# Gated mixing in a two-layer convolution kernel: one image per tile against two images per tile

## The chip, the core and the metric

The kernel runs on one core of one Trainium2 chip. The metric is device time in microseconds (us), taken from the start of the program to its end on that core; lower is better.

## The reference

The input `x` is (8, 64, 256, 256) in float32: 8 images of 64 channels. Two layers follow each other, each as `x = x + layer(groupnorm(x))`.

- Layer 0 shifts four quarters of the channels of two projections by one pixel (one projection first along rows, the other first along columns), weighs them by a softmax gate that is computed for each image from sums over the image, projects the result by a 64x64 matrix, and multiplies it by `sigmoid(scale * x + bias) * x`. All linear parts fold into one small matrix for each image and each of four one-pixel shifts. What is left per pixel is: four shifted 64x64 products, summed; plus a constant; times the sigmoid; plus 1; times the centred input.
- Layer 1 keeps 64x32 Fourier modes of each image, mixes the channels of each mode by complex weights, transforms back and adds.

## The kernel before

The program is a row of stages with a barrier between them: statistics of `x` (DVE and ACT read all of it), a chain of small matrix steps that ends in `wall` (the folded matrices) and `params` (scales and biases), the **mixing stage** (layer 0, lines 511 to 741), a short stage that turns the sums of the mixing stage into the second norm (745 to 793), the forward transform, the mixing of modes, and the backward transform with the last addition. Only the mixing stage and the addresses of what it writes change here.

**The mixing stage before.** It takes one image after the other, 16 rows at a time: 128 tiles. Of a tile, `mix_x` (`XT`, four buffers) holds 17 rows of 257 columns on 128 partitions. The lower 64 partitions hold the 64 channels shifted by one column, the upper 64 the same channels shifted by one row. A matmul with 128 input partitions so takes two of the four shifts at a time, and `m` in 0, 1 takes both pairs. Two output halves (even and odd rows, `par`) fill the 128 partitions of PSUM.

- SP (sync) loads the two halves of a tile by a transfer each onto 64 partitions (564, 567), four tiles ahead, and waits for `conv_done` and `sig_done` of the tile that had the buffer.
- DVE copies what the other half needs: `up` (686), eight rows to the upper partitions, and `down` (691), eight rows to the lower ones, two tiles ahead. It then has the two fused steps of the tile: `gated` (721) reads the matmul's PSUM and the sigmoid, and `mix_out` (730) reads two SBUF tiles and also sums its result. In every second tile it makes half of the centred input (699).
- POOL pads the two edge columns after `down` (589), by two small operations.
- PE runs 16 products of 512 columns (32 matmul instructions) per tile (617), after `padded` and after `gated` of two tiles before has freed the PSUM half.
- ACT makes the centred input (640, one or two halves), the sigmoid (648), issues the store of the finished tile (661) and squares it for the second norm (666).

The order on each engine is written out by hand: in step n, DVE runs up(n+2), gated(n), down(n+2), mix_out(n) and at every second tile centre(n+2); ACT runs gate(n+2), store(n), square(n). The 32 tiles of an image pair are one body of a hardware loop (three rounds, and a last one apart).

Of the kernel before, what the change touches and what calls it, by code (L numbers as in the profile page):

```python
# [42 lines left out]
MR = 2 * SP_  # L43

LAYOUT = ((0, 0, 2), (1, 0, 1), (0, 1, 0), (1, 1, 3))
PITCH = W + 1
# [10 lines left out]
def constants():  # L57
# [23 lines left out]
    put("spread", spread.reshape(P, -1))  # L81
    put("sign", np.stack([np.where(p < C, 1.0, -1.0)] * 2, 1))
# [31 lines left out]
def program(nc, x, w1m, b1m, w2m, b2m, sa1, sa2, gamma, beta, wr1, wi1, wr2, wi2, const, out):  # L114
    top = ExitStack()
    with top:
# [3 lines left out]
        x1 = nc.dram_tensor("x1_scratch", (B, H, C, W), F32, kind="Internal").ap()  # L120
# [7 lines left out]
        x1_rows = x1.rearrange("b h c w -> h b (c w)")  # L128
# [21 lines left out]
        params = sb(top, "params", [P, B + 1, 4])  # L150
        wall = sb(top, "wall", [P, B + 1, P])
# [7 lines left out]
        with ph:  # L159
# [40 lines left out]
            with nc.Block() as block:  # L200
# [12 lines left out]
                def _(pool):  # L213
# [13 lines left out]
                    pool.memset(wall[:, B, :], 0.0)  # L227
                    pool.memset(params[:, B, :], 0.0)
# [283 lines left out]
        with ph:  # L512
            NX = 4
            XT = [sb(ph, f"mix_x{i}", [P, MR + 1, PITCH]) for i in range(NX)]
            XC = [sb(ph, f"centred{i}", [P, SC]) for i in range(NX)]
            G = [sb(ph, f"gated{i}", [P, SC]) for i in range(NX)]
            XO = [sb(ph, f"mix_out{i}", [P, SC]) for i in range(2)]
            SQ = sb(ph, "square", [P, SC])
            one = sb(ph, "one", [P, MR + 1])
            wcur = [sb(ph, f"wcur{i}", [P, P]) for i in range(2)]  # L520
            pcur = [sb(ph, f"pcur{i}", [P, 6]) for i in range(2)]
            loaded = [sem(f"mix_loaded{i}") for i in range(NX)]
            stored = [sem(f"mix_stored{i}") for i in range(2)]
            one_set = sem("mix_one_set")
            doubled, padded, batch_ready = sem("mix_doubled"), sem("mix_padded"), sem("mix_batch_ready")
            xc_done, sig_done, conv_done, sq_done = (sem("mix_" + n) for n in ("xc", "sig", "conv", "sq"))
            h_done, o_done, xc_dve = sem("mix_h"), sem("mix_o"), sem("mix_xc_dve")
            NB = H // MR
            NI = 2 * NB
            ITER = B // 2  # L530

            x1_par = x1.rearrange("b (r e) c w -> b (e c) r w", e=2)

            def split(n):

                return n % 2 == 1

            def loaded_by(i, n):

                q, t = n % NX, n % NB  # L540
                edge = 16 if q in (0, NX - 1) else 0
                batch = NB // NX * 32 + edge
                return i * (2 * batch) + n // NB * batch + (t // NX + 1) * 32 + (edge if q == 0 or t == NB - 1 else 0)

            def iterations(engine, body):

                with engine.Fori(0, ITER - 1) as i:
                    body(i, False)
                body(ITER - 1, True)

            with nc.Block() as block:
                @block.sync
                def _(sp):
                    with sp.Fori(0, ITER) as i:
                        for n in range(NI):
                            ch = bass.ds((i * 2 + n // NB) * C, C)
                            t, xt = n % NB, XT[n % NX]


                            sp.wait_ge(conv_done, i * NI + n + 1)  # L560
                            sp.wait_ge(sig_done, i * NI + n + 1)
                            r0 = t * MR - 1
                            lo = max(r0, 0)
                            sp.dma_start(xt[0:C, lo - r0:MR // 2 + 1, 1:W + 1],
                                         x_rows[ch, lo:r0 + MR // 2 + 1, :]).then_inc(loaded[n % NX], 16)
                            hi = min(r0 + MR + 2, H)
                            sp.dma_start(xt[C:P, MR // 2:hi - r0 - 1, 0:W],
                                         x_rows[ch, r0 + 1 + MR // 2:hi, :]).then_inc(loaded[n % NX], 16)
# [800 lines left out]
```

## Time and profile before

| what | value |
|---|---|
| median of 3 runs | 3113.48 us (3108.65 to 3118.16) |
| the profiled execution's own time | 3114.35 us |
| its span, first to last instruction | 3112.7 us |
| busy in the span: PE, DVE, ACT, POOL | 72%, 65%, 42%, 24% |
| mean granted TensorE clock | 0.930 |

The span is 1.65 us shorter than the execution's own time, which lies 0.9 us over the median. Busy shares are means over stages with different limits, so the profile is to be read stage by stage: the mixing stage lasts from about 380 us to 1462 us of the span.

### The profile page before, as it was taken

To read this page: it belongs to the slowest core of one execution; us is meant where nothing else is said; L and a number is where in the kernel's file an instruction comes from. 1 tells how busy PE (TensorE), PEld (TensorE's weight loads), DVE (VectorE), ACT (ScalarE), POOL (GpSimd) and SP (SyncE) were. 2 spreads that over 40 slices of the span, in tenths; PEclk is the share of its full clock that TensorE was granted. 3 is DMA by queue.
4 is the path that set the end of the run, shared out by engine and by line. 5 is a ranking of instruction groups with operands and counts; after the bars stand their busy time and mean duration, and the time that the engine had idled before them with its cause. 6 is when DMAs were issued, how large, how long until landed. Compare 5 with 4: busy or idle time off the path is not lost. (4 is left out here: it accounts for less than half of the span.)

```text
span 3112.7 us, 38323 instructions
## 1 busy us (share of the span) xinstructions
PE 2255.8 (72%) x12960; PEld 1076.6 (35%) x12960; DVE 2025.2 (65%) x2317; ACT 1302.1 (42%) x1470; POOL 757.3 (24%) x477
## 2 busy tenths in 40 slices
PE   0000288888889889896899898965555989988884
PEld 0000123222223223232345444534555444444442
DVE  8999689989999999997665555640000454544442
ACT  1111078878887888886332222310001222212220
POOL 1000023222323232322655454510000111111111
PEclk9999899999999999998999999987888999998987
DMA  9999299999999999997877676739999999999999
GB/s 402 428 428 428 70 254 264 269 249 276 269 267 257 273 275 267 270 271 215 346 258 260 238 259 243 258 95 347 355 342 317 362 384 395 394 378 409 401 376 351
DMA packets 456398, 949.63 MB, mean 305 GB/s; under 512 B 16608, under 2 KB 377744, under 8 KB 410928
## 3 DMA queue, kind: packets, MB, share of 16 engines
q1 hardware_dynamic: 250720, 619.62, 61.8%
q10 hardware_dynamic: 169984, 192.95, 19.5%
q0 software_dynamic: 35536, 134.84, 11.5%
q8 instruction: 113, 1.85, 0.2%
q14 instruction: 45, 0.37, 0.0%
HBM read 653.75 MB, written 293.60 MB: 304 GB/s over the span
## 5 line engine op out<-in xcount | busy, mean ns | idle before, releaser
L617 PE MATMUL psum<-mix_x,wcur 128*64 128x512 f32 x4096 | 938.1, 614 | 148.6 <-POOL mix_x L589 137.4
L617 PEld LDWEIGHTS psum<-mix_x,wcur 128*64 128x64 f32 x4096 | 311.9, 139 | 774.2 <-issue 564.8
L1227 PE MATMUL psum<-tab_irow_icol_sign,inv_t 128*128 128x512 f32 x1024 | 497.0, 609 | 15.7 <-DVE weights_or_rows L1322 15.1
L589 POOL TENSOR_TENSOR mix_x<-mix_x,one 64x17 f32<-64x17 f32 x256 | 324.0, 1266 | 745.6 <-DVE mix_x L691 738.1
L640 ACT ACTIVATE centred<-mix_x,pcur 64x2048 f32<-64x2048 f32 x192 | 384.2, 2001 | 205.2 <-POOL mix_x L589 188.5
L1322 DVE TENSOR_TENSOR weights_or_rows<-weights_or_rows,psum 128x1024 f32<-128x1024 f32 x224 | 272.7, 1221 | 265.7 <-PE psum L1227 228.5
L983 ACT ACTIVATE fwd_rows<-psum 128x512 f32<-128x512 f32 x256 | 152.2, 598 | 414.6 <-PE psum L869 384.8
L730 DVE SCALAR_TENSOR_TENSOR mix_out<-gated,centred 128x2048 f32<-128x2048 f32 x128 | 293.6, 2294 | 39.4 <-issue 35.2
L264 DVE BATCH_NORM_STATS2 stats<-stat_x 128x6 f32<-128x512 f32 x512 | 305.4, 676 | 13.4 <-DMA stat_x<-x 13.0
L721 DVE SCALAR_TENSOR_TENSOR gated<-psum,pcur,gated 128x2048 f32<-128x2048 f32 x128 | 300.9, 2351 | 18.0 <-PE psum L617 16.4
L1052 DVE COPY fwd_cols<-psum 128x136 f32<-128x136 f32 x512 | 154.6, 394 | 237.8 <-PE psum L880 236.7
L869 PE MATMUL psum<-fwd_sum,tab_ident_frow_fcol 128*64 128x512 f32 x512 | 282.5, 635 | 28.4 <-POOL fwd_diff L1077 18.5
L1291 ACT ACTIVATE inv_t<-psum 128x256 f32<-128x256 f32 x256 | 98.4, 384 | 477.3 <-PE psum L1218 477.3
L869 PE MATMUL psum<-fwd_diff,tab_ident_frow_fcol 128*64 128x512 f32 x512 | 282.8, 636 | 0.0
L1077 POOL TENSOR_TENSOR fwd_diff<-fwd_x 128x2048 f32<-128x2048 f32 x48 | 224.3, 4673 | 239.1 <-PE psum L869 205.6
L648 ACT ACTIVATE gated<-centred,pcur 128x2048 f32<-128x2048 f32 x128 | 268.2, 2095 | 9.6 <-DVE centred L699 1.8
L1202 PE MATMUL psum<-weights_or_rows,modes_or_terms 128*16 128x64 f32 x4096 | 170.3, 354 | 135.3 <-DMA modes_or_terms<-modes_in 111.8
L1227 PEld LDWEIGHTS psum<-tab_irow_icol_sign,inv_t 128*128 128x128 f32 x1024 | 199.5, 196 | 164.8 <-issue 146.1
L666 ACT ACTIVATE square<-mix_out 128x2048 f32<-128x2048 f32 x128 | 242.4, 1894 | 3.6 <-DVE mix_out L730 3.6
L296 PE MATMUL psum<-s_ones_dmask_spread_npix,w1d 128*64 128x128 f32 x1 | 0.4, 396 | 333.7 <-PEq L200 333.7
L1218 PE MATMUL psum<-tab_irow_icol_sign,modes_or_terms 128*128 128x256 f32 x512 | 159.7, 396 | 97.1 <-ACT modes_or_terms L1285 97.1
L1334 POOL DMA_DIRECT2D out<-weights_or_rows x112 | 98.7, 886 | 463.6 <-DMA out<-weights_or_rows 229.3
(185 smaller groups left out, 1982.4 us busy)
## 6 DMA issues: line engine op xcount, KB each, us to landing
mix_x<-x SPq DMA_DIRECT2D x240, 576.0 KB, 8.0
stat_x<-x SPq DMA_DIRECT2D x64, 2048.0 KB, 13.0
x_scratch<-mix_out ACTq DMA_DIRECT2D x128, 1024.0 KB, 9.1
weights_or_rows<-x_scratch SPq DMA_DIRECT2D x112, 1024.0 KB, 10.9
out<-weights_or_rows POOLq DMA_DIRECT2D x112, 1024.0 KB, 16.5
fwd_x<-x_scratch SPq DMA_DIRECT2D x96, 1024.0 KB, 6.8
x_tile<-x_scratch SPq DMA_DIRECT2D x46, 1024.0 KB, 8.0
weights_or_rows<-L_conv_w_real SPq DMA_DIRECT2D x8, 4096.0 KB, 34.3
```

The lines of the kernel that those rows point to most:

```text
L264: last = nc.vector.bn_stats(stats[:, at:at + 6], XT[t % NX][:, q * 512:(q + 1) * 512])
L589: last = nc.gpsimd.tensor_tensor(XT[n % NX][h, :, to], XT[n % NX][h, :, of], one[h, :], ALU.mult)
L617: last = nc.tensor.matmul(bank(k * 4 + q, 512, C, par * C), wcur[j][:, m * C:(m + 1) * C], XT[n % NX][:, r0:r0 + 3:2, m:m + W], start=(m = ...
L640: last = nc.scalar.activation(XC[n % NX][h, :].rearrange("p (r w) -> p r w", w=W), XT[n % NX][h, 1:MR:2, 1 - half:1 - half + W], ACT.Ident ...
L648: nc.scalar.activation(G[n % NX][:, :], XC[n % NX][:, :], ACT.Sigmoid, bias=pcur[j][:, 1:2], scale=pcur[j][:, 0:1]).then_inc(sig_done, 1)
L666: nc.scalar.activation(SQ[:, :], XO[k][:, :], ACT.Square, accum_out=sqs[:, bass.ds(i * NI + n, 1)]).then_inc(sq_done, 1)
L721: nc.vector.scalar_tensor_tensor(out=G[n % NX][:, :], in0=psum[:, k * SC:(k + 1) * SC], scalar=pcur[j][:, 3:4], in1=G[n % NX][:, :], op0=A ...
L730: nc.vector.scalar_tensor_tensor(out=XO[k][:, :], in0=G[n % NX][:, :], scalar=1.0, in1=XC[n % NX][:, :], op0=ALU.add, op1=ALU.mult, accum_ ...
L869: last = nc.tensor.matmul(bank(n % 2, 512, C, par * C), frow[:, par, :], ED[G0 % 2][par][:, 2 * cp:2 * cp + 2, :], start=True, stop=True)
L1077: nc.gpsimd.tensor_tensor(ED[G0 % 2][1][:, :, :], XW[G0 % NX][:, 0, :, :], XW[G0 % NX][:, 1, :, :], ALU.subtract).then_inc(diff_done, 1)
L1227: last = nc.tensor.matmul(bank(n % 2 * 2 + a), TS[n % 2][:, a * P:(a + 1) * P], icol, start=True, stop=True)
L1322: nc.vector.tensor_tensor(xw, xw, psum[:, n % 2 * 1024:n % 2 * 1024 + 1024] .rearrange("p (a k) -> p a k", a=2), ALU.add).then_inc(added, 1)
```

## The change

A tile of the mixing stage is now 8 rows of two images, and there are still 128 of them.

- One transfer of 10 rows on all 128 partitions loads both images into `U` (six buffers, rows of 258 columns): image 0 on the lower 64 partitions, image 1 on the upper.
- Image 0 is multiplied from `U`, whose upper half is overwritten by a copy of its lower half shifted by one row and column (`double`, DVE, 64 partitions x 2321 elements). Image 1 is multiplied from `V` (four buffers): its lower half is a copy of `U`'s upper half by ACT (`low`, 64x2322), its upper half the shifted copy by POOL (`up`, 64x2321).
- The centred input is made by DVE alone, 128x2048 at once (`centre`); ACT has no part in it any more. It has to be made before `double` overwrites half of `U`.
- POOL pads both edge columns by one operation, from `U`, after the load.
- `up(n)` and `low(n)` wait for `conv_done` of tile n-4, which had the same `V`. `double(n)` waits for `centre(n)`, `low(n)` and `up(n)`.
- Results are written over `gated`, the square over `centred`; `mix_out` and `square` have no tiles of their own.
- DVE's order in step n: gated(n), centre(n+2), double(n+2), mix_out(n). ACT's: store(n-1), sigmoid(n+1), square(n-1), low(n+3). POOL's: pad(n+1), up(n).
- All loops of the stage are written out, so there is no jump back.
- The scratch tensor in HBM is laid out by pair, row, image, channel; what reads it later reads runs of the same length.

```diff
-            XT = [sb(ph, f"mix_x{i}", [P, MR + 1, PITCH]) for i in range(NX)]
+            U = [sb(ph, f"mix_u{i}", [P, OWN * PITCH]) for i in range(NU)]
+            V = [sb(ph, f"mix_v{i}", [P, TAPS * PITCH]) for i in range(NV)]
...
+                    for n in range(NI):
+                        q, t = n // NB, n % NB
+                        pair, u = slice(q * P, (q + 1) * P), rows_of(U[n % NU])
+                        if n >= NU:
+                            sp.wait_ge(conv_done, n - NU + 1)
+                        r0 = t * SP_ - 1
+                        lo, hi = max(r0, 0), min(r0 + OWN, H)
+                        sp.dma_start(u[:, lo - r0:hi - r0, 1:W + 1],
+                                     x_rows[pair, lo:hi, :]).then_inc(loaded[n % NU], 16)
...
+                    def pad(n):
+                        pool.wait_ge(loaded[n % NU], loaded_by(n))
+                        if n >= 2:
+                            pool.wait_ge(up_done, n - 1)
+                        u = rows_of(U[n % NU])
+                        nc.gpsimd.tensor_tensor(u[:, :, 0:W + 2:W + 1], u[:, :, 1:W + 1:W - 1], one[:, :, :],
+                                                ALU.mult).then_inc(padded, 1)
+                    def up(n):
+                        pool.wait_ge(padded, min(n + 2, NI))
+                        if n >= NV:
+                            pool.wait_ge(conv_done, n - NV + 1)
+                        k = TAPS * PITCH - 1
+                        nc.gpsimd.tensor_copy(V[n % NV][C:P, 0:k], U[n % NU][C:P, SHIFT:SHIFT + k]).then_inc(up_done, 1)
+                    pad(0)
+                    for n in range(NI):
+                        if n + 1 < NI:
+                            pad(n + 1)
+                        up(n)
...
+                        pe.wait_ge(doubled, n + 1)
+                        if n >= 2:
+                            pe.wait_ge(h_done, n - 1)
+                        taps = (rows_of(U[n % NU]), rows_of(V[n % NV]))
+                        for m in range(2):
+                            for q in range(4):
+                                for e in range(2):
+                                    r0 = 1 - m + q * 2
+                                    last = nc.tensor.matmul(bank(k * 4 + q, 512, C, e * C),
+                                                            wcur[j][:, e, m * C:(m + 1) * C],
+                                                            taps[e][:, r0:r0 + 2, m:m + W],
+                                                            start=(m == 0), stop=(m == 1))
...
+                    def low(n):
+                        act.wait_ge(padded, n + 1)
+                        if n >= NV:
+                            act.wait_ge(conv_done, n - NV + 1)
+                        k = TAPS * PITCH
+                        nc.scalar.activation(V[n % NV][0:C, 0:k], U[n % NU][C:P, 0:k], ACT.Copy).then_inc(low_done, 1)
...
+                    for n in range(NI):
+                        if n >= 1:
+                            store(n - 1)
+                        if n + 1 < NI:
+                            gate(n + 1)
+                        if n >= 1:
+                            square(n - 1)
+                        if n + 3 < NI:
+                            low(n + 3)
...
+                    def centre(n):
+                        dve.wait_ge(loaded[n % NU], loaded_by(n))
+                        if n >= 4:
+                            dve.wait_ge(sq_done, n - 3)
+                        nc.vector.tensor_scalar(XC[n % 4][:, :].rearrange("p (r w) -> p r w", w=W),
+                                                rows_of(U[n % NU])[:, 1:SP_ + 1, 1:W + 1],
+                                                pcur[j][:, 4:5], None, ALU.add).then_inc(xc_done, 1)
+                    def double(n):
+                        dve.wait_ge(xc_done, n + 1)
+                        dve.wait_ge(low_done, n + 1)
+                        dve.wait_ge(up_done, n + 1)
+                        k = TAPS * PITCH - 1
+                        nc.vector.tensor_copy(U[n % NU][C:P, 0:k], U[n % NU][0:C, SHIFT:SHIFT + k]).then_inc(doubled, 1)
...
+                    for n in range(NI):
+                        dve.wait_ge(conv_done, n + 1)
+                        dve.wait_ge(sig_done, n + 1)
+                        nc.vector.scalar_tensor_tensor(out=G[n % 4][:, :], in0=psum[:, k * SC:(k + 1) * SC], ...
+                        if n + 2 < NI:
+                            centre(n + 2)
+                            double(n + 2)
+                        dve.wait_ge(h_done, n + 1)
+                        nc.vector.scalar_tensor_tensor(out=G[n % 4][:, :], in0=G[n % 4][:, :],
+                                                       scalar=1.0, in1=XC[n % 4][:, :], ...
```

In the short stage behind it, one matmul of the sums becomes two and two small copies become four.

## Rows read from the trace of the kernel before

**Rows 1.** Stages by window: first the view's own names of its columns.

```profile
core 0: us, PE busy (x) PEld busy (x) DVE busy (x) ACT busy (x) POOL busy (x), PEclk, DMA share, GB/s
380.00:1480.00 1100.00, 940.50 (x4114) 314.01 (x4114) 995.36 (x738) 892.08 (x579) 324.02 (x256) 0.95 1.03 262
```

**Rows 2.** Groups by line: names, shapes, count | busy us, mean ns | idle before, releaser.

```profile
L721 DVE SCALAR_TENSOR_TENSOR gated<-psum,pcur,gated 128x2048 f32<-128x2048 f32 x128 | 300.9, 2351 | 18.0 <-PE psum L617 16.4
L730 DVE SCALAR_TENSOR_TENSOR mix_out<-gated,centred 128x2048 f32<-128x2048 f32 x128 | 293.6, 2294 | 39.4 <-issue 35.2 <-DMA x_scratch<-mix_out 1.3
L691 DVE COPY mix_x<-mix_x 64x2048 f32<-64x2048 f32 x128 | 156.7, 1224 | 4.0
L686 DVE COPY mix_x<-mix_x 64x2048 f32<-64x2048 f32 x128 | 156.2, 1221 | 24.4 <-DMA mix_x<-x 14.9 <-issue 5.1
L699 DVE TENSOR_SCALAR centred<-mix_x,pcur 64x2048 f32<-64x2048 f32 x64 | 82.4, 1287 | 2.1
...
L640 ACT ACTIVATE centred<-mix_x,pcur 64x2048 f32<-64x2048 f32 x192 | 384.2, 2001 | 205.2 <-POOL mix_x L589 188.5 <-issue 15.7
L648 ACT ACTIVATE gated<-centred,pcur 128x2048 f32<-128x2048 f32 x128 | 268.2, 2095 | 9.6 <-DVE centred L699 1.8
L666 ACT ACTIVATE square<-mix_out 128x2048 f32<-128x2048 f32 x128 | 242.4, 1894 | 3.6 <-DVE mix_out L730 3.6
```

**Rows 3.** Timeline (start us, us, what): the first and the last of 128 `gated` steps.

```profile
401.40 2.35 DVE L721 SCALAR_TENSOR_TENSOR gated<-psum,pcur,gated 128x2048 f32<-128x2048 f32 x1
...
1455.31 2.35 DVE L721 SCALAR_TENSOR_TENSOR gated<-psum,pcur,gated 128x2048 f32<-128x2048 f32 x1 [2.59 <-PE psum L617]
```

**Rows 4.** Timeline of DVE, POOL and PE over two tiles of the mixing stage.

```profile
450.40 2.35 DVE L721 SCALAR_TENSOR_TENSOR gated<-psum,pcur,gated 128x2048 f32<-128x2048 f32 x1
...
454.04 2.29 DVE L730 SCALAR_TENSOR_TENSOR mix_out<-gated,centred 128x2048 f32<-128x2048 f32 x1
454.09 3.59 POOL L589 TENSOR_TENSOR mix_x<-mix_x,one 64x17 f32<-64x17 f32 x2 [9.41 <-DVE mix_x L691]
...
456.38 1.22 DVE L686 COPY mix_x<-mix_x 64x2048 f32<-64x2048 f32 x1
457.61 2.35 DVE L721 SCALAR_TENSOR_TENSOR gated<-psum,pcur,gated 128x2048 f32<-128x2048 f32 x1
...
457.74 14.49 PE L617 MATMUL psum<-mix_x,wcur 128*64 128x512 f32 x56 [4.39 <-POOL mix_x L589]
...
461.30 0.51 POOL L589 TENSOR_TENSOR mix_x<-mix_x,one 64x17 f32<-64x17 f32 x2 [3.61 <-DVE mix_x L691]
```

**Rows 5.** One line, `pad` (589): min/median/max ns of one.

```profile
L589 POOL TENSOR_TENSOR mix_x<-mix_x,one x256: 221/1208/2377, 390.1 to 1446.8; 64x17 f32<-64x17 f32 x128
```

**Rows 6.** Timeline of POOL and DVE in the forward transform.

```profile
1595.05 2.27 DVE L1007 TENSOR_TENSOR fwd_sum<-fwd_x 128x2048 f32<-128x2048 f32 x1
...
1595.66 6.04 POOL L1077 TENSOR_TENSOR fwd_diff<-x_tile 128x2048 f32<-128x2048 f32 x1 [1.69 <-PE psum L869]
...
1611.65 4.52 POOL L1077 TENSOR_TENSOR fwd_diff<-fwd_x 128x2048 f32<-128x2048 f32 x1 [1.83 <-PE psum L869]
...
1612.18 1.39 DVE L1052 COPY fwd_cols<-psum 128x136 f32<-128x136 f32 x4 [0.97 <-PE psum L880]
1613.42 4.90 DVE L1007 TENSOR_TENSOR fwd_sum<-fwd_x 128x2048 f32<-128x2048 f32 x1
```

**Rows 7.** Timeline: the last tile's matmuls on PE.

```profile
1448.15 7.11 PE L617 MATMUL psum<-mix_x,wcur 128*64 128x512 f32 x32 [0.17 <-POOL mix_x L589]
```

**Rows 8.** DMA queues, 20 us of the stage: GB/s in 40 slices, queues, issues.

```profile
GB/s 381 391 385 381 309 246 211 203 203 231 213 225 297 348 389 385 387 373 381 363 291 199 205 205 238 209 213 217 219 274 377 385 385 334 354 348 225 199 209 182
...
x_scratch<-mix_out ACTq DMA_DIRECT2D x3, 1024.0 KB, 10.2
mix_x<-x SPq DMA_DIRECT2D x4, 576.0 KB, 8.9
```

More of the change, by code:

```diff
@@ L81, in constants @@
     put("spread", spread.reshape(P, -1))
+    both = np.stack([0.5 * ((p[:, None] // C == d) & (c[:, None] // 2 == c[None, :] // 2)) for d in range(2)], 1)
+    put("both", both.reshape(P, -1))
     put("sign", np.stack([np.where(p < C, 1.0, -1.0)] * 2, 1))
@@ L512, in program @@
         with ph:
-            NX = 4
-            XT = [sb(ph, f"mix_x{i}", [P, MR + 1, PITCH]) for i in range(NX)]
[L515 to L520, printed above, removed]
+            NU, NV = 6, 4
@@ L545, in iterations, with rows_of, loads_of @@
[L545 to L549, printed above, removed]
+            h_done, o_done = sem("mix_h"), sem("mix_o")
+            NB = H // SP_
+            NI = NQ * NB
+            SHIFT = PITCH + 1
+            x1_out = x1.rearrange("q h e c w -> q (e c) h w")
+            def rows_of(t):
+                return t[:, :].rearrange("p (r w) -> p r w", w=PITCH)
+            def loads_of(n):
+                return 2 if n % NB in (0, NB - 1) else 1
@@ L551, in program, with loaded_by @@
+            def loaded_by(n):
+                return 16 * sum(loads_of(m) for m in range(n % NU, n + 1, NU))
             with nc.Block() as block:
@@ new lines, in square @@
+                    def square(n):
+                        nc.scalar.activation(XC[n % 4][:, :], G[n % 4][:, :], ACT.Square,
+                                             accum_out=sqs[:, n:n + 1]).then_inc(sq_done, 1)
+                    for n in range(3):
+                        low(n)
+                    gate(0)
+                    for n in range(NI):
[7 more added lines that the diff above has]
+                            low(n + 3)
@@ L744, in program @@
         ph = ExitStack()
         with ph:
-            T = table(ph, ["group", "ident"])
+            T = table(ph, ["both", "ident"])
             sv = sb(ph, "norm2_values", [P, 10, B])
@@ L751, in _ @@
                 def _(sp):
-                    for n in ("group", "ident"):
+                    for n in ("both", "ident"):
                         sp.dma_start(*T[n]).then_inc(n2_tab, 16)
@@ L762, in _ @@
                     pe.wait_ge(n2, 2)
-                    nc.tensor.matmul(bank(0, 2 * B), T["group"][0], sv[:, 2:4, :].rearrange("p a b -> p (a b)"),
-                                     start=True, stop=True).then_inc(n2, 1)
+                    for d in range(2):
+                        last = nc.tensor.matmul(psum[:, d * 1024:d * 1024 + 2 * NQ], T["both"][0][:, d * P:(d + 1) * P],
+                                                sv[:, 2, :], start=True, stop=True)
+                    last.then_inc(n2, 1)
                 @block.scalar
```

239 lines of the change are left out of this document (71 added, 168 removed).

## Prediction

> **What bounds the kernel now.** The stages are apart, so I read the mixing stage alone. The table by windows shows that there no engine is full: in 1100 us DVE is busy 995, PE 940, ACT 892 [rows 1]. The groups by line give the work of one tile on each [rows 2]. DVE: 2.35 + 2.29 + 1.22 + 1.22 + half of 1.29 = 7.73 us. ACT: 1.5 x 2.00 + 2.10 + 1.89 = 6.99. The first and the last of the 128 gated steps start 1053.9 us apart [rows 3], so a tile takes 1053.9 / 127 = **8.30 us**. The 0.57 us above DVE's own work is the gaps between its instructions and a loop of waits: pad is late, so ACT's centring is late (188.5 us idle behind the pad), then the sigmoid and the square, for which mix_out waits (35.2 us).
>
> Why pad is late decides this case. The timeline shows two pads issued together with mix_out, which take 3.59 us; the same two take 0.51 us when DVE is quiet [rows 4]. One pad takes 0.22 us at the least and 2.38 at the most [rows 5]. The 3.59 us end at 457.68, just behind mix_out (456.33) and the copy after it (457.60). So POOL stands still while DVE runs an operation with two SBUF inputs or a copy from SBUF to SBUF, and it gets in as such an operation ends. It holds in the other direction too: in the forward transform a DVE addition that takes 2.27 us takes 4.90 when POOL's subtraction (1611.65 to 1616.17) is already running [rows 6]. Less its 2.27 us of work, the addition ran from 1616.05: POOL gives the port back 0.12 us before its own end. The subtraction behind the addition took 6.04; 4.5 us before its end is 1597.2, 0.1 us before the addition ends at 1597.32. DVE copies that read PSUM run beside POOL's 4.52 us untouched. I call this "the port": one of the two has it for a whole instruction.
>
> **The change part by part, for one tile.**
>
> DVE loses up and down (2 x 1.22) and the half-tile centring, and gets a whole centring every tile: 1.29, as the time goes by elements per partition, and double: 1.22 x 2321/2048 = 1.39. The cycle from 450.40 to 457.61 has 7.21 us for 7.08 us of work [rows 4], so 0.13 us of gaps. New cycle: 2.35 + 1.29 + 1.39 + 2.29 + 0.13 = **7.45 us**, 0.85 under the present 8.30.
>
> ACT: copy low 2.00 x 2322/2048 = 2.27 in place of 3.00 of centring; 2.27 + 2.10 + 1.89 = 6.26 us. It is covered by DVE's 7.45, and the pad no longer stands ahead of the sigmoid. Were DVE's cycle under 6.3, ACT would be the bound by the difference. The store moves behind mix_out at once, ahead of the sigmoid; its issue lies beside ACT's work.
>
> PE: the same 32 instructions, 7.11 us for a tile by itself [rows 7]. Covered, with 0.34 us to spare.
>
> DMA: loads grow from 1.18 to 1.31 MB per tile, with 1.05 MB of stores 2.36 MB. The rate swings today between about 200 GB/s (loads onto 64 partitions) and 385 (with a store) [rows 8]. At 348 to 385 GB/s the new tile takes 6.1 to 6.8 us: covered. At 268, the rate that today's 2.23 MB in 8.30 us make, it would be 8.8; I take the higher rate, as the slices show it with stores running. SP issues one transfer instead of two; loads are issued six tiles ahead and take about 9 us to land. Free.
>
> POOL: one pad and up, 64x2321, each tile. The trace has no such copy. From below, a pass at ACT's 0.83 ns per element (1.89 us less some 0.2, over 2048): 2321 x 0.83 + 0.22 = 2.15 us. From above, all that POOL's two-input subtraction takes, (4.52 - 0.22)/2048 = 2.10 ns each: 5.1 us. If each operand is half of that, as one input is read instead of two, 2.66 us. I take **2.4**, between the lower end and that half, since it is a one-input pass; 2.15 and 5.1 stay for the range. What a page has on this: the Trainium skill, "GPSIMD Engine Reference", section 3.1, has 1.03 cycles per element for light bodies, which at its 1.2 GHz is an estimate of 2.0 us plus the start, and the sum by it would be some 25 us lower than mine; the same page puts this work better on DVE.
>
> Where does up fall? gated reads PSUM and one SBUF tile; by the copies from PSUM [rows 6] I take it as leaving the port free. The other three, centring, double, mix_out (4.97 us), take it. Up would be free if it ran under gated's 2.35 us. But it is started by something else: up(n) waits for conv_done(n-4), since it writes the V of that tile. PE starts a tile when its double ends (0.05 us later, as it starts 0.06 after the pad in [rows 4]), takes 7.11, and POOL follows 0.05 to 0.09 after (gated followed PE by 0.05 at the last tile, 1455.26 to 1455.31 [rows 3, 7]). So up asks for the port 7.21 to 7.25 us after the end of a double. The next mix_out starts 7.45 us after it. POOL is 0.2 us early: it asks while the next double is running, and gets in between double and mix_out, as the pad did between mix_out and copy. DVE then waits for up: it gets the port late by 2.4 - 0.05 (granted as it stands) - 0.12 (early release) - 0.12 (granted before DVE's end, and the gap) = **2.1 us**. In the next cycle that mix_out is later, so the request falls 2.3 us ahead of double's end, in the centring (it occupies 2.7 to 1.4 us ahead): up gets in behind it and double waits 2.1 us. Then it repeats. Every tile pays; nothing pulls it back into gated's time. The pad, behind its up, asks while DVE holds the port and slips into a gap: 0.06 us.
>
> Sum: 7.45 + 2.1 + 0.06 = 9.61 us; (9.61 - 8.30) x 127 = **+166 us**. Round it: the first tile waits for pad(1) and up before its double, where before it had two DVE copies, about +3; batch changes are 3 instead of 7, of twice the work, 0; the short stage behind gets one matmul and two copies, +0.6. The stalls at the jumps back (the loops are written out now) are in the 8.30 already and not in 9.61. Other stages keep their lengths of runs: 0. 3114.35 + 170 = **3284 us**; the profiled execution is 0.9 us over the median, so nothing changes by going to it.
>
> **Rivals.**
>
> *The copy falls under gated* (0.35). If PE's tile takes 0.2 us more, or a double 0.1 less on either side of my sums, up asks after mix_out has the port, gets it at mix_out's end, and 2.1 to 2.4 us fit into gated's 2.35. It stays there, because a cycle without stall keeps the phase. For it: the margin is 0.2 us, and the low clock in short stretches lengthens PE's tile (mean 0.95 [rows 1]). Against it: any stall on DVE makes the request earlier. Time: 7.45 to 7.5 us per tile, 127 x 0.83 = -105, +4: about 3013. This is the other side.
>
> *POOL copies at the two-input rate* (0.05). 5.1 us: mix_out waits 4.8; the next request falls into the start of gated, and centring waits 2.5; on average 3.7, tile 11.2: +368, 3483. For: the subtraction is the only large operation of POOL in the trace. Against: it reads two operands, the copy one.
>
> *Double isn't two-wide* (0.05). 2321 is odd, and mix_out's pace of 1.12 ns per element would make it 2.6 us. Then it needs no port, the cycle is 8.66, and up mostly runs beside double; stalls of 0.4 to 0.75 on average give 9.1 us: +105, 3219. The Trainium skill, "VectorE: DVE Perf Modes", section "Mode 2×_2P", allows an odd length if it is equal on both sides, which it is here; no row here has an odd one.
>
> *The two orders mix* (0.05), with the phase broken by clock and batch changes: about 8.3 us per tile, no difference.
>
> A rule that speaks against the change is in the Trainium skill, "SBUF — State Buffer", section "Who interferes with whom": whichever instruction comes first has the shared port pair to its end, and the other blocks. By rows 4 and 6 the trace agrees; by that rule alone (one input, no two-port mode) gated leaves it free.
>
> **How the numbers follow.** Forecast 0.50, then 0.35, 0.05, 0.05, 0.05. The point is the likeliest case's. Its own range, for a copy of 2.15 to 2.9 us, is 3250 to 3350. Faster and slower hold most of the chance together, so the range of all cases reaches from 3000 (the copy hidden, with some of the jump stalls gained) to 3390; the 5.1 us case lies outside. A measurement of this kernel tells 0.3% (9 us) from no change: faster 0.35, same 0.05, slower 0.60.
>
> **What would show it.** Up's record should last 2.2 to 2.7 us when it meets no one. Mix_out near 4.4 us and double near 3.5 should take turns from tile to tile, the other of the two at its 2.29 or 1.39, and gated should stay 2.35 with starts 9.6 us apart; PE should wait for double. Wrong: mix_out at 2.29 throughout and starts 7.5 us apart (the hidden case), double at 2.6 throughout, gated longer than 2.35 (it takes the port too), DVE idle before gated for PE or before centring for a load.

## The result and the profile after

The changed kernel takes **3007.78 us** where 3284 was forecast (median of 4 runs, 3001.52 to 3008.3), the one before 3115.82 beside it. The ratio is 0.9651, with a 95% interval of 0.9629 to 0.9674: faster by 3.5%. The profiled execution took 3008.19 us, its span is 3006.2. The case that I had put second, the copy under `gated`, priced at 3013, is the one that came.

The time came from the mixing stage. Timeline, the first and the last of the 128 `gated` steps of the changed kernel (start us, us, what), to be held against [rows 3]:

```profile
402.29 2.35 DVE L708 SCALAR_TENSOR_TENSOR gated<-psum,pcur,gated 128x2048 f32<-128x2048 f32 x1 [5.06 <-PE psum L612]
...
1338.76 2.35 DVE L708 SCALAR_TENSOR_TENSOR gated<-psum,pcur,gated 128x2048 f32<-128x2048 f32 x1 [0.26 <-PE psum L612]
```

They are 936.47 us apart, against 1053.91 before: 7.37 us per tile in place of 8.30, 117.4 us less. The span is only 106.5 us shorter, because the stages behind took 10 us longer in this execution (from the first addition of the forward transform to the end, 1640.9 us against 1631.3). In the eleven profiled executions below that stretch lies between 1629 and 1640 with nothing in it changed. Why it varies is open, and so up to 10 us of a difference between two run times may belong to it. That is why I compare the distance of the `gated` steps from here on, and the run times beside it.

Groups by line of the changed kernel, as [rows 2] shows them for the one before (`mix_out` now has the buffer of `gated`, so L716 is the `mix_out` step; L695 is double, L685 centring, L589 up, L580 pad, L626 the copy to the low half, L635 the sigmoid):

```profile
L716 DVE SCALAR_TENSOR_TENSOR gated<-gated,centred 128x2048 f32<-128x2048 f32 x128 | 302.7, 2365 | 4.0
L589 POOL COPY mix_v<-mix_u 64x2321 f32<-64x2321 f32 x128 | 302.3, 2362 | 35.4 <-PE psum L612 27.8
L708 DVE SCALAR_TENSOR_TENSOR gated<-psum,pcur,gated 128x2048 f32<-128x2048 f32 x128 | 300.3, 2346 | 5.6 <-PE psum L612 5.3
L626 ACT ACTIVATE mix_v<-mix_u 64x2322 f32<-64x2322 f32 x128 | 274.0, 2141 | 37.8 <-POOL mix_u L580 34.8
L635 ACT ACTIVATE gated<-centred,pcur 128x2048 f32<-128x2048 f32 x128 | 268.1, 2095 | 165.2 <-DVE gated L716 165.2
...
L695 DVE COPY mix_u<-mix_u 64x2321 f32<-64x2321 f32 x128 | 178.3, 1393 | 11.4 <-POOL mix_v L589 7.0
L685 DVE TENSOR_SCALAR centred<-mix_u,pcur 128x2048 f32<-128x2048 f32 x128 | 168.1, 1313 | 5.4 <-DMA mix_u<-x 5.4
```

DVE waits for almost nothing now (4.0, 5.6, 11.4 and 5.4 us over 128 tiles), and ACT, which was late before, waits for DVE (165.2 us). `mix_out` has a mean of 2365 ns: 2293 in nearly all tiles and about 4090 in a few. The timeline of DVE and POOL shows the common tile:

```profile
858.97 1.36 DVE L695 COPY mix_u<-mix_u 64x2321 f32<-64x2321 f32 x1
...
860.36 2.29 DVE L716 SCALAR_TENSOR_TENSOR gated<-gated,centred 128x2048 f32<-128x2048 f32 x1
860.43 2.32 POOL L580 TENSOR_TENSOR mix_u<-mix_u,one 128x20 f32<-128x20 f32 x1 [2.69 <-DMA mix_u<-x]
...
862.58 2.35 DVE L708 SCALAR_TENSOR_TENSOR gated<-psum,pcur,gated 128x2048 f32<-128x2048 f32 x1
862.81 2.12 POOL L589 COPY mix_v<-mix_u 64x2321 f32<-64x2321 f32 x1
...
864.85 1.28 DVE L685 TENSOR_SCALAR centred<-mix_u,pcur 128x2048 f32<-128x2048 f32 x1
866.16 1.36 DVE L695 COPY mix_u<-mix_u 64x2321 f32<-64x2321 f32 x1
...
867.55 2.29 DVE L716 SCALAR_TENSOR_TENSOR gated<-gated,centred 128x2048 f32<-128x2048 f32 x1
```

The cycle is 7.19 us. The pad of the next tile waits for its load, which lands while `mix_out` runs; it stands still there until `mix_out` ends. Up, behind it in POOL's queue, starts 0.23 us into `gated` and ends with it: it costs DVE nothing. Of the 127 distances of `gated`, 109 are 7.2 us. Most of the others lie behind the first tile and behind tiles 16, 48 and 80. In those three tiles DVE copies the matrices and parameters of the next pair of images, behind `mix_out` and 16 tiles ahead of their use. I call these the batch copies. One of them meets up itself: up, which elsewhere runs beside `gated`, has the port from 526.72 on, and the copy takes 2.15 us and not 0.25. Timeline:

```profile
526.49 0.25 DVE L673 COPY wcur<-wall 128x128 f32<-128x128 f32 x1
...
526.79 2.15 DVE L673 COPY wcur<-wall 128x128 f32<-128x128 f32 x1
```

Some tiles behind the batch copies show what I had forecast for every tile:

```profile
766.82 1.36 DVE L695 COPY mix_u<-mix_u 64x2321 f32<-64x2321 f32 x1
766.97 3.20 POOL L589 COPY mix_v<-mix_u 64x2321 f32<-64x2321 f32 x1
768.22 4.09 DVE L716 SCALAR_TENSOR_TENSOR gated<-gated,centred 128x2048 f32<-128x2048 f32 x1
...
775.48 2.28 POOL L589 COPY mix_v<-mix_u 64x2321 f32<-64x2321 f32 x1 [2.75 <-PE psum L612]
775.81 3.17 DVE L695 COPY mix_u<-mix_u 64x2321 f32<-64x2321 f32 x1
```

Up gets in between double and `mix_out`, and `mix_out` takes 1.80 us more (4.09 for 2.29); in the next tile up gets in behind the centring, and double takes 1.81 more (3.17 for 1.36). So the mechanism exists. What had to be found out is why it is the exception, and where the 0.93 us per tile (8.30 - 7.37) came from.

### The profile page after: what moved, and what is told of

It reads as the page before. It is cut to its first block and busy times, and to the rows that moved or that the text cites. A ratio compares the mean times of both kernels' runs of the same rounds, so it can differ in the third digit from the quotient of the medians.

```text
span 3006.2 us, 36702 instructions
## 1 busy us (share of the span) xinstructions
PE 2235.7 (74%) x12962; PEld 1052.0 (35%) x12962; DVE 1969.1 (66%) x2252; ACT 1195.9 (40%) x1406; POOL 883.0 (29%) x475
## 5 line engine op out<-in xcount | busy, mean ns | idle before, releaser
L612 PE MATMUL psum<-mix_u,wcur 128*64 128x512 f32 x2048 | 914.1, 600 | 54.9 <-DVE mix_u L695 44.6
L612 PE MATMUL psum<-mix_v,wcur 128*64 128x512 f32 x2048 | 914.2, 600 | 0.0
L612 PEld LDWEIGHTS psum<-mix_u,wcur 128*64 128x64 f32 x2048 | 271.4, 137 | 683.3 <-issue 552.9
L635 ACT ACTIVATE gated<-centred,pcur 128x2048 f32<-128x2048 f32 x128 | 268.1, 2095 | 165.2 <-DVE gated L716 165.2
L589 POOL COPY mix_v<-mix_u 64x2321 f32<-64x2321 f32 x128 | 302.3, 2362 | 35.4 <-PE psum L612 27.8
L716 DVE SCALAR_TENSOR_TENSOR gated<-gated,centred 128x2048 f32<-128x2048 f32 x128 | 302.7, 2365 | 4.0
L626 ACT ACTIVATE mix_v<-mix_u 64x2322 f32<-64x2322 f32 x128 | 274.0, 2141 | 37.8 <-POOL mix_u L580 34.8
L580 POOL TENSOR_TENSOR mix_u<-mix_u,one 128x20 f32<-128x20 f32 x128 | 147.6, 1153 | 450.2 <-DMA mix_u<-x 447.3
L612 PEld LDWEIGHTS psum<-mix_v,wcur 128*64 128x64 f32 x2048 | 271.3, 137 | 0.0
```

The costliest lines, as they stand in the source:

```text
L589: nc.gpsimd.tensor_copy(V[n % NV][C:P, 0:k], U[n % NU][C:P, SHIFT:SHIFT + k]).then_inc(up_done, 1)
L612: last = nc.tensor.matmul(bank(k * 4 + q, 512, C, e * C), wcur[j][:, e, m * C:(m + 1) * C], taps[e][:, r0:r0 + 2, m:m + W], start=(m == 0) ...
L626: nc.scalar.activation(V[n % NV][0:C, 0:k], U[n % NU][C:P, 0:k], ACT.Copy).then_inc(low_done, 1)
L635: nc.scalar.activation(G[n % 4][:, :], XC[n % 4][:, :], ACT.Sigmoid, bias=pcur[j][:, 1:2], scale=pcur[j][:, 0:1]).then_inc(sig_done, 1)
L716: nc.vector.scalar_tensor_tensor(out=G[n % 4][:, :], in0=G[n % 4][:, :], scalar=1.0, in1=XC[n % 4][:, :], op0=ALU.add, op1=ALU.mult, accum ...
```

## The experiments

All ratios are to the kernel before, run on the same chip (medians of 3110.47 to 3115.25 us). "Distance" is from one start of `gated` to the next, "mean" the mean distance.

**1. Put the copy where it must collide.** Up of tile n also waits for the centring of tile n-2. Double of that tile follows it on DVE, so up asks as that double starts.

```
                         if n >= NV:
                             pool.wait_ge(conv_done, n - NV + 1)
+                            pool.wait_ge(xc_done, n - 1)
```

> The changed kernel with one wait more: POOL's copy up(n) also waits for the centring of tile n-2 (xc_done), so that it always asks for the port while double runs. Nothing is left out. If the port is one owner's for a whole instruction and goes to the one who asked first, up runs between double and mix_out in every tile: mix_out's record 2.29 + 1.80 = 4.09 us (as in the few tiles of the changed kernel where it happens), tiles 7.19 + 1.80 = 8.99 us apart, in all (8.99 - 7.37) x 127 = +206 us, about 3214 us. If up costs nothing wherever it falls (rival: my port price was wrong and not only the phase), the time stays at 3008 us within 10.

Measured: 3200.22 us, ratio 1.0275 [1.0251, 1.0299]; the distance of `gated` is 8.99 us in the common tile. Timeline:

```profile
866.38 1.36 DVE L696 COPY mix_u<-mix_u 64x2321 f32<-64x2321 f32 x1
866.51 3.22 POOL L590 COPY mix_v<-mix_u 64x2321 f32<-64x2321 f32 x1 [3.54 <-DVE centred L686]
867.78 4.09 DVE L717 SCALAR_TENSOR_TENSOR gated<-gated,centred 128x2048 f32<-128x2048 f32 x1
...
871.80 2.34 DVE L709 SCALAR_TENSOR_TENSOR gated<-psum,pcur,gated 128x2048 f32<-128x2048 f32 x1
```

The port and its price are as the forecast had them: 8.99 - 7.19 = 1.80 us per tile, and the kernel becomes slower than the one before. The same instructions take 192 us more than in the changed kernel when up's record starts 1.27 us ahead of `mix_out`'s start and not 2.45 behind it. The Trainium skill has the rule ("SBUF — State Buffer", section "Who interferes with whom": the first to come keeps the shared ports to its end); the trace agrees, with 1.80 us lost to a copy of 2.12.

**2. Take away the load's landing, which holds up back.** POOL's order is turned, up(n) and then pad(n+1), so up no longer stands behind a pad that waits for a load inside `mix_out`.

```
-                        pool.wait_ge(padded, min(n + 2, NI))
+                        pool.wait_ge(padded, n + 1)
...
                     for n in range(NI):
+                        up(n)
                         if n + 1 < NI:
                             pad(n + 1)
-                        up(n)
```

> The changed kernel with POOL's order turned: up(n), then pad(n+1), so that up(n) waits for conv_done(n-4) alone and no longer for the pad of the next tile and with it for that tile's load. Nothing is left out. Theory A (the landing of the load holds up back until mix_out has the port; without it up comes too early, in the double): every tile pays 1.8 us, 8.99 us apart, about 3214 us. Theory B (the cycle is 7.19 us and not 7.45, so that the end of the matmuls, about 7.25 us after a double, already falls behind the start of the next mix_out at 7.22): period stays 7.19, 3008 us or up to 20 us less, as late and early landings no longer move up.

Measured: 2986.8 us, ratio 0.9582 [0.9566, 0.9598], mean 7.29. Timeline:

```profile
861.21 1.36 DVE L695 COPY mix_u<-mix_u 64x2321 f32<-64x2321 f32 x1
862.60 2.29 DVE L716 SCALAR_TENSOR_TENSOR gated<-gated,centred 128x2048 f32<-128x2048 f32 x1
862.67 4.21 POOL L589 COPY mix_v<-mix_u 64x2321 f32<-64x2321 f32 x1 [2.61 <-PE psum L612]
...
864.82 2.35 DVE L708 SCALAR_TENSOR_TENSOR gated<-psum,pcur,gated 128x2048 f32<-128x2048 f32 x1
```

Without that hold up still comes late enough: 0.07 us behind the start of `mix_out`. It then waits out `mix_out` (record 4.21 us) and runs under `gated`. So theory B holds for the common tile, and the margin is seven hundredths of a microsecond. It is the same in most tiles: in 95 of the 128 up's record begins 0.06 or 0.07 us behind a start of `mix_out`. The double of the tile before ended at 861.21 - 7.19 + 1.36 = 855.38; up asks 7.29 us after that, and `mix_out` starts 7.22 after it. That is the comparison on which the forecast hung, with 7.21 to 7.25 and 7.45 in it.

**3. Leave the copy out.** POOL makes no up at all. The upper half of V is set to zero once, so a part of the convolution's input is missing; double waits for the pad in its place.

```
                         if n + 1 < NI:
                             pad(n + 1)
-                        up(n)
...
-                        dve.wait_ge(up_done, n + 1)
+                        dve.wait_ge(padded, n + 1)
```

> The changed kernel without POOL's copy up: the upper half of V is zero throughout (so image 1 of each pair lacks two of its four shifts), double waits for the pad in its place. By the port theory the copy costs the changed kernel only what its 11 long DVE records and late tiles show: starts of gated 7.19 us apart throughout, at most (7.37 - 7.19) x 127 = 23 us less, 2985 to 3000 us. A rival that puts more on POOL (the copy slows PE, ACT or DMA, or the first tile's start) expects under 2980.

Measured: 2977.25 us, ratio 0.9551 [0.9535, 0.9567]. The common tile stays at 7.19 and the mean becomes 7.19, against 7.37 with the copy: (7.37 - 7.19) x 127 = 23 us of the changed kernel are tiles in which up stands in DVE's way, and the batch copies cost 0.78 us without it (7.97 for 7.19) where they cost 2.73 with it (9.92). The run is 30.5 us shorter (the spans of the profiled executions differ by 23.8). By its time alone the run lies below the 2985 to 3000 that I expected, and below the 2980 of the rival. The distances speak against the rival: they give exactly the 23 us of the expectation, and nothing in the common tile. Where the other 7 us lie is not shown; the profiled execution took 2984.1 us, the other three 2974.7 to 2977.5.

**4. What do the jumps back cost?** The kernel before, with its loops written out and nothing else.

```
-                with engine.Fori(0, ITER - 1) as i:
-                    body(i, False)
-                body(ITER - 1, True)
+                for i in range(ITER):
+                    body(i, i == ITER - 1)
...
```

> The kernel before with the loops of its mixing stage written out on all engines, nothing else. Theory: of the 0.26 us by which my cycle for DVE was too long, most is the gap between its instructions, which is shorter where waits and addresses are constants (0.13 us of gaps before, less than none after), and the three jumps back cost about 16 us: 127 x 0.2 + 16 = 41 us less at most, 3070 to 3100 us, since the loop through pad and ACT still bounds the tile. Rival: written-out loops give nothing (instruction fetch in place of the jumps): 3115 us within 10, and the whole gain is the new split of work.

Measured: 3095.91 us, ratio 0.993 [0.9913, 0.9948]; mean distance 8.15 us in place of 8.30. So 19 us of the 117 belong to the loops. Most of it is at the three jumps: the distances across them were 16.51, 15.24 and 10.95 us, and are 8.53, 8.52 and 9.07 now. The gaps between DVE's instructions stayed as they were, 2.38 us from a start of `gated` to the next start, so the idea that straight code closes them fell.

**5. What do the pads cost?** The written-out kernel of experiment 4, and without the copying of the edge columns: they stay zero, so the output's edges differ, and PE and ACT wait for the doubling itself.

```
-                            last = nc.gpsimd.tensor_tensor(XT[n % NX][h, :, to], XT[n % NX][h, :, of],
-                                                           one[h, :], ALU.mult)
...
-                            pe.wait_ge(padded, i * NI + n + 1)
+                            pe.wait_ge(doubled, i * NI + n + 1)
```

> The kernel before with its loops written out, and GpSimd's copying of the edge columns left out (the edge columns stay zero, so the output's edge columns differ); matmuls and the low-half copy wait for the doubling itself. Theory A, that in the kernel before the DVE order of two tiles costs 7.20 us of DVE time in one tile and 8.52 in the next only because the pads are late by the port: every tile goes down to DVE's own cycle, 7.2 to 7.4 us, and the run takes 3096 - (8.15 - 7.3) x 127 = 2988 us (2975 to 3000). Theory B, that the even tile's 8.52 us comes from the order itself (DVE alternates, and something other than the pads is late, as PE's matmuls behind the doubling): it stays within 15 us of the 3096 us that the written-out kernel took.

Measured: 3057.41 us, ratio 0.9827 [0.9798, 0.9855]; mean distance 7.85, alternating 7.21 and 8.53. Timeline:

```profile
867.55 2.35 DVE L711 SCALAR_TENSOR_TENSOR gated<-psum,pcur,gated 128x2048 f32<-128x2048 f32 x1
869.93 1.22 DVE L681 COPY mix_x<-mix_x 64x2048 f32<-64x2048 f32 x1
871.18 2.29 DVE L720 SCALAR_TENSOR_TENSOR mix_out<-gated,centred 128x2048 f32<-128x2048 f32 x1
...
873.52 1.29 DVE L689 TENSOR_SCALAR centred<-mix_x,pcur 64x2048 f32<-64x2048 f32 x1
874.84 1.22 DVE L676 COPY mix_x<-mix_x 64x2048 f32<-64x2048 f32 x1
876.07 2.35 DVE L711 SCALAR_TENSOR_TENSOR gated<-psum,pcur,gated 128x2048 f32<-128x2048 f32 x1
```

Both theories missed, and both from one oversight: 8.53 is 7.21 plus the centring that DVE does for two tiles every second tile (1.32 from start to start). Neither port nor PE is in it. DVE's own cycle before was (7.21 + 8.53) / 2 = 7.87 us, and the pads, late by the port, cost 8.15 - 7.85 = 0.30 us per tile.

**6. How thin is the margin?** The order of experiment 2, with a spare memset on DVE behind each `mix_out`.

```
+            spare = sb(ph, "spare", [P, 192])
...
+            nc.vector.memset(spare[:, :], 0.0)
```

> e2's kernel (up ahead of pad) with one more small DVE instruction per tile, a memset of 128x192 elements of a spare tile between mix_out and gated: about 0.26 us, which makes DVE's cycle the 7.45 us that I had forecast. Nothing is left out. Theory B (up asks about 7.25 us after a double; it was 0.07 us behind the start of mix_out in e2): with 7.45 it asks 0.2 us ahead of it, gets in behind the double, and every tile costs 7.45 + 1.80 = 9.25 us: about 3236 us, or down to 3150 if stretches of low clock put it back under gated for a while. Rival (the phase is kept by something else, and a longer cycle only adds itself): 2987 + 33 = 3020 us.

Measured: 3062.75 us, ratio 0.9843 [0.9801, 0.9885]; mean 7.83. I had meant the memset to add 0.26 us and bring the cycle to 7.45, but it adds 0.09 (7.28). The run fits neither expectation (3150 to 3236 us, or 3020). The 0.09 us make 11 us over 127 tiles, and the run is 76 us longer than in experiment 2. The distances repeat in groups of seven, 7.28 five times, then 9.23 and 9.08. By the numbers of experiment 2 `mix_out` now starts 7.31 us behind the double and up still asks at 7.29: it is early by 0.02. The comparison of the forecast decides between 7.19 and 7.28 as it should. But only two tiles of seven pay.

**7. The changed kernel with the same memset.**

> The changed kernel itself (pad of the next tile ahead of up) with the same memset. Nothing is left out. Theory C: here up also waits for the load of the next tile, which is issued at the end of the matmuls of tile n-5 and lands some 8 us later, that is after the end of those of n-4; this would have hidden up even with my cycle of 7.45: most starts 7.45 us apart, 3008 + 33 = 3041 us, up to 3100. If the landing is no guard: as e5, 3150 to 3240 us.

Measured: 3018.98 us, ratio 0.9695 [0.9654, 0.9736], mean 7.48: 11 us over the changed kernel, what the memset itself costs. Here the pad that waits for the load does hold up back: up's record begins within 0.3 us behind the start of `mix_out` or 2.45 behind it in 109 of the 128 tiles, and ahead of it in 8.

**8. Is it the moment of the copy?** Experiment 6, with a wait that lets up start only when the `mix_out` ahead of `gated` is done.

```
         def up(n):
             if n >= NV:
                 pool.wait_ge(conv_done, n - NV + 1)
+                pool.wait_ge(o_done, n - NV)
```

> e5's kernel (with the memset) and one wait: up(n) also waits for mix_out of tile n-5 (o_done), so that it can't ask before gated runs. Nothing is left out. If the phase alone decides, every tile takes 7.45 us and the late tiles behind a change of image pair go too: 2987 + 33 - 10 = 3010 us. If something else in e5 costs the time, it stays as slow as e5.

Measured: 2996.29 us, ratio 0.9634 [0.9592, 0.9676], mean 7.33. One wait on POOL gives 66 us back of the 76, with the same work on every engine. The 3010 us of the expectation again had the memset at 0.26 us.

**9. A cycle as long as the forecast had it.** Experiment 6 with 448 columns. The cycle is 7.54 us, 0.09 over the 7.45 of the forecast.

> The order up(n), pad(n+1), with a spare memset of 448 columns of 128 partitions behind each mix_out in place of 192, to bring DVE's own cycle to about the 7.45 us that the forecast took for the changed kernel. Theory A, the forecast's (the upper-half copy is early by the surplus in every pair of tiles, and nothing pulls it back): the mean distance of gated is 7.4 + 1.8 or more, so about 9.1 us, and the run 3260 us (2987 + (9.1 - 7.29) x 127 = 3217 at the least). Theory B, from the run with 192 columns (each stall leaves the matmuls at a lower granted clock for some microseconds, so that the copy is late again and needs several tiles to come early): with a surplus of about 0.25 us a tile instead of 0.08 it comes early sooner, in every third or fourth tile: mean 7.4 + 1.8 x 2 / 5 = 8.1, the run 3090 us (3050 to 3150).

Measured: 3119.51 us, ratio 1.0029 [1.0014, 1.0044], mean 8.31. The distances repeat: 7.54 three times, then 9.35 twice. POOL's timeline over one such group (L590 is up; in brackets, POOL's idle time and what ended it):

```profile
857.20 2.64 POOL L590 COPY mix_v<-mix_u 64x2321 f32<-64x2321 f32 x1 [3.07 <-PE psum L613]
...
870.05 2.86 POOL L590 COPY mix_v<-mix_u 64x2321 f32<-64x2321 f32 x1 [8.90 <-PE psum L613]
...
876.91 3.54 POOL L590 COPY mix_v<-mix_u 64x2321 f32<-64x2321 f32 x1 [3.62 <-PE psum L613]
...
883.78 4.21 POOL L590 COPY mix_v<-mix_u 64x2321 f32<-64x2321 f32 x1 [2.95 <-PE psum L613]
...
890.98 2.23 POOL L590 COPY mix_v<-mix_u 64x2321 f32<-64x2321 f32 x1 [2.60 <-PE psum L613]
...
898.52 2.63 POOL L590 COPY mix_v<-mix_u 64x2321 f32<-64x2321 f32 x1 [3.07 <-PE psum L613]
```

Against the starts of `mix_out` (868.64, 876.18, 883.72, 891.26) up comes 1.41, 0.73, 0.06 us late, then 0.28 early: there `mix_out` takes 4.09, and in the next tile double 3.17. Behind the two stalls PE has stood still, and it comes back at half clock. The matmul and the table by windows (engines' busy us, then the granted clock) show it:

```profile
861.12 1.03 PE L613 MATMUL psum<-mix_u,wcur 128*64 128x512 f32 x1 [4.06 <-DVE mix_u L696]
```

```profile
core 0: us, PE busy (x) PEld busy (x) DVE busy (x) ACT busy (x) POOL busy (x), PEclk, DMA share, GB/s
...
861.00:863.00 2.00, 1.88 (x6) 0.66 (x8) 1.97 (x2) 0.00 (x0) 0.15 (x1) 0.56 0.85 288
863.00:865.00 2.00, 2.00 (x7) 0.50 (x6) 1.96 (x4) 1.09 (x1) 0.00 (x0) 0.59 0.36 127
865.00:867.00 2.00, 2.00 (x12) 0.71 (x10) 2.00 (x2) 2.00 (x2) 0.00 (x0) 1.00 1.09 387
```

In these 4 us the windows have a granted clock of 0.56 to 0.59, near the 1.2 GHz level. PE starts 13 matmuls where 24 would fit, so its tile lasts 8.8 us and not 7.1, and up is late again. Then PE catches up, because its tiles run 6.87 us apart while DVE's run 7.54, and gains 0.67 us per tile until up is early. The slow matmuls behind a stall are what pulls the copy back. That they are the cause is read from the rows; no run tries the clock alone. In this run the stage has 27 such stops of 4.06 us or more, and behind each of them the granted clock is low for some microseconds. In experiment 1, where PE stops for 1.90 us per tile, the granted clock fell only three times in the whole stage (at 562, 678 and 1138 us, for some 4 us each), and every tile pays.

**10. The changed kernel with 448 columns.**

> The changed kernel itself (pad first) with the same spare memset of 448 columns. If the landing of the load, on which the pad waits inside mix_out, still holds the upper-half copy back in steady tiles, the run costs only what the memset adds over the changed kernel: about (7.4 - 7.19) x 127 = 27 us, 3035 us (3025 to 3060). If the landing no longer does (the load has more time in a longer cycle, so it lands earlier against mix_out), the stalls spread over the tiles as in the other order, 3100 us or more.

Measured: 3082.49 us, ratio 0.989 [0.986, 0.9921], mean 8.05. That is between the two theories. At 7.54 us the load's landing still holds up back in most tiles, but in 31 of the 128 up's record begins ahead of `mix_out`'s start (8 in experiment 7), and stalls come in groups all through the stage. As a guard the load is an accident of timing.

**11. A better version.** Experiment 2 with the wait of experiment 8, without the memset; PE takes its weights from the table of all batches, and the small parameters are set ahead for all four, so there are no batch copies in the row of tiles.

```
-            pcur = [sb(ph, f"pcur{i}", [P, 6]) for i in range(2)]
+            pcur = [sb(ph, f"pcur{i}", [P, 6]) for i in range(NQ)]
...
+                pool.wait_ge(o_done, n - NV)
...
-                                     wcur[j][:, e, m * C:(m + 1) * C],
+                                     wall[:, n // NB * 2 + e, m * C:(m + 1) * C],
```

> e2's kernel with the same wait for mix_out of tile n-5, without the memset, and without the copies at a change of image pair: PE takes its weights from wall itself, and the scales and biases of all four pairs are set ahead of the first tile. Nothing is left out. Starts of gated 7.19 us apart throughout: 2987 - (7.29 - 7.19) x 127 = 2974 us, 0.4% under e2 and 1.1% under the changed kernel. If the waits cost DVE or POOL anything: at or above 2987.

Measured: **2975.96 us** (6 runs, 2972.7 to 2980.65), ratio 0.9559 [0.9528, 0.9591]. Timeline:

```profile
859.37 2.29 DVE L714 SCALAR_TENSOR_TENSOR gated<-gated,centred 128x2048 f32<-128x2048 f32 x1
...
861.58 2.35 DVE L706 SCALAR_TENSOR_TENSOR gated<-psum,pcur,gated 128x2048 f32<-128x2048 f32 x1
861.83 2.12 POOL L589 COPY mix_v<-mix_u 64x2321 f32<-64x2321 f32 x1 [3.80 <-DVE gated L714]
```

Up is released by `mix_out` in every tile, and all distances but the first and the last are 7.19 (mean 7.18). This kernel beats both, and takes what the one without any copy took (2977.25).

## Where the 117 us came from, and why the prediction was wrong

The runs divide the gain. From 8.30 us per tile: the loops written out, 0.15 (19 us, experiment 4); the pads no longer in the way, 0.30 (38 us, experiment 5); DVE's shorter cycle, 7.85 to 7.19 (83 us). Of these 0.66 us per tile, 0.45 is less work (the records sum to 7.73 before and 7.28 after), and the rest is shorter gaps between the records. Given back are 23 us in which up stands in DVE's way.

**Right.** The changed kernel is DVE's: what it waits for is gone, and PE, ACT and the loads are covered. The port is held by one engine for a whole instruction, in both directions. A stall was forecast at 2.1 us and is 1.80; the difference is the copy, 2.12 us where I took 2.4. My lower bound of 2.15 lay a little high, and was the nearest of my three values. The estimate by the Trainium skill, "GPSIMD Engine Reference", section 3.1 (2.0 us plus the start), was nearer than the 2.4 that I took, and the trace's 2.12 us agrees with it within 0.1 us. The copy to the low half took 2.14 against 2.27, double 1.36 against 1.39, centring 1.28 against 1.29. Double is two-wide with an odd length: 1.36 us, not the 2.6 of the rival. The stall's path, first between double and `mix_out`, then between centring and double, is in the trace as it was written. The price of the second case, 3013, is 5 us off, and that is in part luck. Its tile was 7.45 to 7.5 us where 7.37 was measured, and the stages behind, which it left alone, took 10 us longer in the profiled execution. Its reason (PE's tile longer or a double shorter by 0.1 to 0.2 us) isn't the one that the runs show either.

**The step that failed** is "new cycle: 2.35 + 1.29 + 1.39 + 2.29 + 0.13 = 7.45", and with it "POOL is 0.2 us early". I took the gaps of the old order, 0.13 us, over to the new one. There they are below nothing: the four records sum to 7.28 us and the cycle is 7.19, since `gated` starts 2.22 us after the start of a `mix_out` that lasts 2.29, and the centring 2.27 after a `gated` that lasts 2.35. With 0.03 us less for double and 0.01 for centring that is the 0.26. Neither pair, `mix_out` then `gated` or `gated` then centring, stands in the order of the kernel before, so its rows couldn't show this. The request was mis-sized too, 7.29 us behind the double where I had 7.21 to 7.25: POOL follows the last matmul's end by 0.15 us (862.52 to 862.67 in experiment 2), and I had taken 0.05 to 0.09 from DVE. So the comparison is 7.29 against 7.22, not 7.23 against 7.45: up is 0.07 late instead of 0.2 early. The margin was smaller than the error of its terms, and I still gave one side 0.50. Between that case and the hidden one no row of before decided, and the chances should have been near equal, or the other way.

**The second step that failed** is "every tile pays; nothing pulls it back". Experiment 9 has a cycle of 7.54 us, longer than the 7.45 of the forecast: two tiles of five pay, and the mean is 8.31, not 9.61. I had held PE's tile at 7.11 us after a stall. At the low clock it is 8.8, and that brings the copy back under `gated` (read from the rows; no run sets the clock). With a cycle near mine the kernel came to 3082.5 us in its own order (experiment 10) and to 3119.5 with up first (experiment 9), and not to 3284. Only where a wait holds the phase, as in experiment 1, does every tile pay its 1.80.

**What I left out**: the pad ahead of up in POOL's queue waits for its load. I costed the loads as "Free" and looked only at whether DVE would wait. In most tiles they land within `mix_out` and hold up back by another 2.4 us. At 7.19 us this wasn't needed (experiment 2); at 7.28 it was worth 65 us (experiments 6 and 7: 76 against 11). It costs something too: with pad first the mean distance is 7.37 us, with up first 7.29 (10 us of the 21 by which the runs differ; where the other 11 lie is not shown), as more tiles are disturbed behind the batch copies.

**Before the change** I explained the time above DVE's work by the pads and the gaps. The pads were 0.30 us per tile, the jumps 0.15. That the even tile's extra 1.3 us was nothing but the half centring stood in my own sum, and I lost sight of it when I wrote the expectation of experiment 5.

## What to carry to other kernels

When two engines share a port, the cost of an operation on the second one is decided by when it is released, not only by how long it takes. Here the same copy costs nothing (experiment 11 against 3), 66 us (6 against 8) or 223 us (1 against 3). Don't leave the moment to chance; name in a wait the instruction behind which the copy should start (here `mix_out`, so that it runs beside the step that reads PSUM). A forecast in which the sign hangs on a difference of 0.2 us between two sums of 7 us has two nearly equal cases, and should be given as such.

## What the hardware showed that I had not expected

- The distance from one DVE instruction's start to the next depends on the pair. `mix_out` to `gated` is 2.21 to 2.22 us, to the memset of 192 columns 2.29, to the memset of 448 columns, an SBUF copy or the half centring 2.33 to 2.35; `gated` to the centring of 128 partitions is 2.27, `gated` to an SBUF copy 2.38. Behind the memset the record of `gated` itself is 2.23 us instead of 2.35, so I read some 0.12 us of its record behind `mix_out` as a start that overlaps. Why centring follows sooner than a copy stays open; the copies go from one half of the partitions to the other, the centring keeps to its own, and no run tries this alone.
- A memset whose record is 0.22 us adds 0.09 us to the cycle, one of 0.43 us adds 0.35. So 0.13 and 0.08 us of the record add nothing.
- A waiting POOL instruction gets in between two DVE instructions whose records are 0.04 us apart (in the changed kernel double ends at 768.18 and `mix_out` starts at 768.22), and DVE loses 1.80 us for a copy of 2.12.
- PE's granted clock was near half for some 4 us behind each of the 27 stops of 4.06 us or more in experiment 9. In experiment 1, with a stop of 1.90 us in nearly every tile, it fell three times in the stage; two of these falls lie behind a longer stop of 2.69 us, and behind a third such stop (at 849.8 us of its span) it stayed at 1.00.
